# First two tiles of x ahead, a separate buffer of empty rows, and expert weights loaded in eight slices, in a transformer block with eight experts

## The reference: one block of attention and experts

```python
mod = (silu(c) @ wmod)                       # sa, ca, ga, sb, cb, gb per sequence
h = layernorm(x) * (1 + ca) + sa
x = x + ga * attention(h)                    # 16 heads, 4 key/value heads, 64 wide, window of 128,
                                             # scores through 30 * tanh(s / 30)
h = layernorm(x) * (1 + cb) + sb
x = x + gb * experts(h)                      # 8 experts of 128 -> 512 -> 128, each token goes to
                                             # the one with the largest gate, at most 512 per expert
```

## Time and profile before

| | |
|---|---|
| median of 3 runs | 476.98 us (475.44 to 479.21) |
| profiled execution | 476.81 us, span 475.1 us |
| mean granted TensorE clock | 0.952 |
| busy: PE, DVE, ACT, POOL | 88%, 60%, 63%, 65% |
| bytes moved | 37.73 MB, of which written to memory 17.31 MB |

### The profile page before, as it was taken

One profiled execution on the slowest core, in us unless ns is written; L12 is line 12 of the kernel. 1 busy time (PEld: TensorE's weight loads), 2 busy tenths in 40 slices (PEclk: granted clock), 3 DMA queues, 4 the chain that ended last, 5 costly groups with the idle time before them and its releaser, 6 DMA issues. The chain is left out here.

```text
span 475.1 us, 14910 instructions
## 1 busy us (share of the span) xinstructions
PE 417.4 (88%) x5608; PEld 294.0 (62%) x5608; DVE 286.9 (60%) x846; ACT 298.0 (63%) x537; POOL 310.8 (65%) x494
## 2 busy tenths in 40 slices
PE   2894999999999999999999999999999742899970
PEld 1652566766767676666677666767565531799960
DVE  6263557775676868576777756675777541245631
ACT  4785457777776868777777778676756221564420
POOL 6136248587786969687867878676769851055572
PEclk9998899999999999999999999999999765999995
DMA  8987000101101010102011110101020125971110
GB/s 261 369 294 231 3 23 3 41 25 37 52 20 54 20 52 20 43 19 70 20 52 38 35 41 21 52 20 52 21 86 24 42 96 188 364 248 39 33 50 16
DMA packets 32078, 37.73 MB, mean 79 GB/s; under 512 B 3474, under 2 KB 28311, under 8 KB 32008
## 3 DMA queue, kind: packets, MB, share of 16 engines
q1 hardware_dynamic: 28936, 28.22, 19.1%
q0 software_dynamic: 3072, 8.56, 5.0%
HBM read 15.88 MB, written 17.31 MB: 70 GB/s over the span
## 5 line engine op out<-in xcount | busy, mean ns | idle before, releaser
L1185 POOL TENSOR_TENSOR OL<-O,OH 128x512 fp32r<-128x512 f32 x64 | 81.3, 1285 | 22.3 <-ACT OH L701 21.8
L865 DVE COPY_PREDICATED own<-before,turns 128x1024 f32<-128x1024 uint32 x56 | 68.8, 1229 | 40.3 <-PE turns L424 40.3
L689 ACT ACTIVATE PR<-own 128x1024 f32<-128x1024 f32 x64 | 65.5, 1024 | 42.4 <-DVE own L865 42.0
L1177 POOL TENSOR_SCALAR_AFFINE_SELECT PM<-PR 128x1024 f32<-128x1024 f32 x64 | 69.5, 1096 | 22.4 <-ACT PR L695 22.0
L695 ACT ACTIVATE PR<-PR 128x1024 f32<-128x1024 f32 x64 | 65.8, 1054 | 0.0
L420 PE MATMUL own<-Q,K 64*32 64x256 f32 (+3 forms) x896 | 58.8, 441 | 1.9 <-ACT PR L689 1.7
L896 DVE TENSOR_TENSOR O<-turns,R 128x512 f32<-128x512 f32 x64 | 41.2, 685 | 29.2 <-PE turns L463 28.9
L424 PE MATMUL turns<-Q,K 64*32 64x128 f32 (+3 forms) x896 | 57.4, 429 | 0.0
L701 ACT ACTIVATE OH<-O 128x512 fp32r<-128x512 f32 x64 | 40.0, 628 | 11.0 <-DVE O L896 10.9
L1221 POOL DMA_INDIRECT sorted_rows<-PAY,slot_i x32 | 35.1, 1096 | 14.0 <-issue 10.9
L424 PEld LDWEIGHTS turns<-Q,K 64*32 64x32 f32 x896 | 36.5, 107 | 9.4
(11 more groups left out here) (189 smaller groups left out, 1010.8 us busy)
## 6 DMA issues: line engine op xcount, KB each, us to landing
sorted_rows<-PAY SPq DMA_DIRECT2D x8, 800.0 KB, 12.1
VM<-V SPq DMA_DIRECT2D x56, 64.0 KB, 2.1
x_sb<-x_dram SPq DMA_DIRECT2D x4, 512.0 KB, 6.7
w_stage<-w_dram SPq DMA_DIRECT2D x1, 2048.0 KB, 10.9
out_dram<-PAY SPq DMA_DIRECT2D x32, 64.0 KB, 1.7
x_sb<-sorted_rows SPq DMA_DIRECT2D x2, 800.0 KB, 9.6
Q<-sorted_rows SPq DMA_DIRECT2D x2, 800.0 KB, 9.1
PR<-sorted_rows SPq DMA_DIRECT2D x2, 800.0 KB
```

The lines of the kernel that those rows point to most:

```text
L689: act.activation(pr, own[:, :, :].rearrange("p a n -> p (a n)"), ACT.Tanh, scale=SCORE_SCALE).then_inc(tanhed, 1)
L865: dve.copy_predicated(own[:, :, :].rearrange("p a (r n) -> p (a r) n", n=P), before[:, :].bitcast(U32).unsqueeze(1).to_broadcast([P, 2 * R ...
L1177: pool.affine_select(out=PM[:, u % P_RING, :].rearrange("p (r n) -> p r n", n=P), in_=PR[:, u % P_RING, :].rearrange("p (r n) -> p r n", n ...
L1185: pool.tensor_tensor(OL[:, t % 2, c, :], O[:, t % 2, c, :], OH[:, t % 2, c, :].bitcast(F32), ALU.subtract).then_inc(ol_done, 1)
```

## The change

The first batch of x is loaded in two parts, two tiles and six tiles. c and wmod are loaded from ScalarE's queue, wmod in two halves, wq in two halves with a semaphore each. The eight blocks of empty rows are issued ahead of wo and of the other three batches of x, and come from a buffer of their own; a row is 388 words long instead of 400. ScalarE normalises tiles 0 and 1 before it splits the query weights, and VectorE makes the first `XL` before it splits the other half of them and the value weights. The first weights of the experts are loaded in eight transfers of one expert each, one in each turn of SyncE's loop from tile 8 on, instead of one transfer before the loop.

```diff
-ROW_H, ROW_G, ROW_X, ROW_ID, ROW = 0, P, 2 * P, 3 * P, 400
+ROW_H, ROW_ID, ROW_G, ROW_X, ROW = 0, P, P + 4, 2 * P + 4, 3 * P + 4
+W1_TILE = 8
-        empty_row = PAY[:, PAY_RING - 1, :]
+        empty_row = sb("empty_row", [P, ROW])
...
-            sp.dma_start(x_sb[:, 0:BATCH_TILES, :], x_v[0]).then_inc(x_in[0], 16)
-            sp.dma_start(cT[:, :], c).then_inc(c_in, 16)
-            sp.dma_start(stage_m, wmod).then_inc(wmod_in, 16)
+            sp.dma_start(x_sb[:, 0:2, :], x_v[0][:, 0:2, :]).then_inc(x_first, 16)
             sp.dma_start(stage_k, wk).then_inc(wk_in, 16)
+            sp.dma_start(stage_q[:, QH:], wq[:, QH:]).then_inc(wq1_in, 16)
+            sp.dma_start(stage_q[:, :QH], wq[:, :QH]).then_inc(wq0_in, 16)
             sp.dma_start(stage_v, wv).then_inc(wv_in, 16)
-            sp.dma_start(stage_q, wq).then_inc(wq_in, 16)
+            sp.dma_start(x_sb[:, 2:BATCH_TILES, :], x_v[0][:, 2:BATCH_TILES, :]).then_inc(x_in[0], 16)
+            sp.wait_ge(consts, CONSTS)
+            for e in range(EXPERTS):
+                sp.dma_start(sorted_v[e], empty_row[:, :].unsqueeze(1).to_broadcast([P, ST, ROW])).then_inc(empty_in, 16)
+            sp.dma_start(stage_o, wo.rearrange("p (i n) -> p i n", n=P)).then_inc(wo_in, 16)
             for b in range(1, BATCHES):
                 sp.dma_start(x_sb[:, b * BATCH_TILES:(b + 1) * BATCH_TILES, :], x_v[b]).then_inc(x_in[b], 16)
-            sp.dma_start(stage_o, wo.rearrange("p (i n) -> p i n", n=P)).then_inc(wo_in, 16)
             sp.dma_start(Wg[:, :], wg).then_inc(rest_in, 16)
             sp.dma_start(b1_col[:, :, :], b1).then_inc(rest_in, 16)
-            sp.wait_ge(consts, CONSTS)
-            for e in range(EXPERTS):
-                sp.dma_start(sorted_v[e], empty_row.unsqueeze(1).to_broadcast([P, ST, ROW])).then_inc(empty_in, 16)
...
-            sp.wait_ge(weights_l, len(split))
-            sp.wait_ge(columns_done, 1)
-            sp.wait_ge(rows_done, 1)
-            sp.dma_start(w1_sb, w1.rearrange("e h f -> h e f")).then_inc(w1_in, 16)
+
+            def load_w1(e):
+
+                if e == 0:
+                    sp.wait_ge(weights_l, len(split))
+                    sp.wait_ge(columns_done, 1)
+                    sp.wait_ge(rows_done, 1)
+                sp.dma_start(w1_sb[:, e, :], w1[e]).then_inc(w1_in, 16)
...
                 if is_tile(e + 24):
                     mix_v(e + 24)
+                if W1_TILE <= e + 14 < W1_TILE + 2 * EXPERTS:
+                    load_w1((e + 14 - W1_TILE) // 2)
...
+            act.dma_start(cT[:, :], c).then_inc(c_in, 16)
+            act.dma_start(stage_m[:, 0:3 * P], wmod[:, 0:3 * P]).then_inc(wmod_in, 16)
+            act.dma_start(stage_m[:, 3 * P:6 * P], wmod[:, 3 * P:6 * P]).then_inc(wmod2_in, 16)
             act.wait_ge(c_in, 16)
             act.activation(c_e[:, :], cT[:, :], ACT.Exp, scale=-1.0).then_inc(c_exped, 1)
             split_high(SPLIT_K)
+            normalise1(0)
+            normalise1(1)
+            split_high(SPLIT_Q1)
+            high_x(0)
             split_high(SPLIT_Q0)
             split_high(SPLIT_V)
-            split_high(SPLIT_Q1)
...
             def measure1(t):
-                dve.wait_ge(x_in[t // BATCH_TILES], 16)
+                dve.wait_ge(x_first if t < 2 else x_in[t // BATCH_TILES], 16)
...
                 if e == -16:
                     keep_columns()
                     split_low(SPLIT_K)
-                    split_low(SPLIT_Q0)
-                    split_low(SPLIT_V)
                     split_low(SPLIT_Q1)
-                    prepare_mod()
                 if is_tile(e + 16):
                     full_x(e // 2 + 8)
                     low_x(e // 2 + 8)
+                if e == -16:
+                    split_low(SPLIT_Q0)
+                    split_low(SPLIT_V)
+                    keep_gate()
+                    prepare_mod()
...
-            pool.memset(PAY[:, :, :], 0.0).then_inc(consts, 1)
+            pool.memset(PAY[:, :, ROW_ID:ROW_G], 0.0).then_inc(consts, 1)
+            pool.memset(empty_row[:, :], 0.0).then_inc(consts, 1)
...
             def scatter(t):
                 r = t % PAY_RING
+                if t == 0:
+                    pool.wait_ge(empty_in, 16 * EXPERTS)
```

More of the change, by code:

```diff
@@ L46 @@
 HOME = {
-    ("columns",): 0, ("rows",): 1,
+    ("columns",): 0, ("rows",): 2,
     ("before", 0, 0): 2, ("before", 0, 1): 2, ("before", 1, 0): 2, ("before", 1, 1): 1,
@@ L185, in build @@
         turns = pb("turns", [P, 6, 512])
+        x_first = sem("x_first")
         x_in = [sem(f"x_in{b}") for b in range(BATCHES)]
-        wk_in, wv_in, wq_in, c_in, wmod_in, wo_in, w1_in, b2_in, rest_in, mod_in = sems(
-            "wk_in", "wv_in", "wq_in", "c_in", "wmod_in", "wo_in", "w1_in", "b2_in", "rest_in", "mod_in")
+        wk_in, wv_in, wq0_in, wq1_in, c_in, wmod_in, wmod2_in, wo_in, w1_in, b2_in, rest_in, mod_in = sems(
+            "wk_in", "wv_in", "wq0_in", "wq1_in", "c_in", "wmod_in", "wmod2_in", "wo_in", "w1_in", "b2_in", "rest_in", "mod_in")
         mod_out, empty_in, row_rest_in = sems("mod_out", "empty_in", "row_rest_in")
@@ L234, in build @@
         split = (
-            (WkH[:, :], WkL[:, :], stage_k), (WqH[:, :QH], WqL[:, :QH], stage_q[:, :QH]), (WvH[:, :], WvL[:, :], stage_v),
-            (WqH[:, QH:], WqL[:, QH:], stage_q[:, QH:]),
+            (WkH[:, :], WkL[:, :], stage_k), (WqH[:, QH:], WqL[:, QH:], stage_q[:, QH:]),
+            (WqH[:, :QH], WqL[:, :QH], stage_q[:, :QH]), (WvH[:, :], WvL[:, :], stage_v),
             (WoH[:, REP:, :], WoL[:, REP:, :], stage_o[:, REP:, :]), (WoH[:, :REP, :], WoL[:, :REP, :], stage_o[:, :REP, :]))
-        SPLIT_K, SPLIT_Q0, SPLIT_V, SPLIT_Q1, SPLIT_O1, SPLIT_O0 = range(6)
-        split_in = (wk_in, wq_in, wv_in, wq_in, wo_in, wo_in)
-        CONSTS = 14
+        SPLIT_K, SPLIT_Q1, SPLIT_Q0, SPLIT_V, SPLIT_O1, SPLIT_O0 = range(6)
+        split_in = (wk_in, wq1_in, wq0_in, wv_in, wo_in, wo_in)
+        CONSTS = 15
         turn_banks = [turns[:, n, :] for n in (0, 1)]
@@ L532, in program_pe @@
             n, ps = take("rows")
+            pe.wait_ge(wmod2_in, 16)
             pe.matmul(ps[0:BATCHES, 0:3 * P], siluT[:, :], stage_m[:, 3 * P:6 * P], start=True, stop=True).then_inc(rows_done, 1)
@@ L722, in gate_row @@
                     act.wait_ge(mod_in, 16)
-                    act.wait_ge(empty_in, 16 * EXPERTS)
                 if t >= PAY_RING:
@@ L751, in program_act @@
                     keep_h2(e + 6)
-                if is_tile(e + 14):
+                if is_tile(e + 14) and e + 14 > 1:
                     high_x(e // 2 + 7)
@@ L778, in program_act @@
                     expose(e + 11, 1)
-                if is_tile(e + 16):
+                if is_tile(e + 16) and e + 16 > 1:
                     normalise1(e + 16)
-                if is_tile(e + 17):
+                if is_tile(e + 17) and e + 17 > 1:
                     normalise1(e + 17)
@@ L820, in relu @@
                     act.activation(hidden[e % 2][:, f, :], up_banks[f], ACT.Relu, bias=b1_col[:, e, f:f + 1]).then_inc(relu_done, 1)
-            act.wait_ge(w1_in, 16)
+            act.wait_ge(w1_in, 16 * EXPERTS)
             act.wait_ge(rest_in, 32)
@@ L904, in add_x @@
                     dve.wait_ge(x1_out[r], 16 * (t // PAY_RING))
-                elif t == 0:
-                    dve.wait_ge(empty_in, 16 * EXPERTS)
                 dve.tensor_tensor(PAY[:, r, ROW_X:ROW_X + P], bank["y", t][:, 0:P], x_sb[:, t, :], ALU.add).then_inc(x1_done, 1)
@@ L976, in keep_columns, with keep_gate @@
                 dve.tensor_scalar(ca_col[:, :], col[:, 4:4 + BATCHES], 1.0, None, ALU.add).then_inc(ca_kept, 1)
+            def keep_gate():
+                col = bank["columns",]
                 dve.tensor_scalar(ga_sign[:, :], col[:, 8:8 + BATCHES], 0.0, 0.5, ALU.is_ge, ALU.subtract).then_inc(ga_signed, 1)
@@ L1140, in program_pool @@
                                pattern=[[-1, P]], channel_multiplier=1).then_inc(consts, 1)
-            pool.wait_ge(consts, 5)
+            pool.wait_ge(consts, 6)
             pool.memset(empty_row[:, ROW_ID:ROW_ID + 1].bitcast(I32), NO_TOKEN).then_inc(consts, 1)
@@ L1144, in program_pool @@
             pool.iota(tok_id[:, :], pattern=[[P, TILES]], base=0, channel_multiplier=1).then_inc(consts, 1)
-            pool.wait_ge(consts, 10)
+            pool.wait_ge(consts, 11)
             pool.tensor_copy(iota8[:, :], iota8i[:, :]).then_inc(consts, 1)
@@ L1211, in name_row @@
                     pool.wait_ge(pay_out[r], 16 * (t // PAY_RING))
-                else:
-                    pool.wait_ge(empty_in, 16 * EXPERTS)
                 pool.tensor_copy(PAY[:, r, ROW_ID:ROW_ID + 1].bitcast(I32), tok_id[:, t:t + 1]).then_inc(id_done, 1)
```

## The result

The changed kernel takes 484.79 us in the median of 4 runs (482.92 to 485.90), the kernel before on the same occasion 476.21. The ratio is 1.0176, 95% interval 1.0142 to 1.0209: it is slower, by 8.4 us if the ratio is applied to the 476.21. The forecast was 479.6 us and no change; the range ended at 484.5.

The account below looks back on a forecast made before the run. TensorE was taken to bound the attention, so head delays reach the end almost whole. A net +2.6 us at attend(1)'s end plus 0.2 for the slices gave +2.8 on 476.81: 479.6 us, no change, range 470 to 484.5.

Parts of the forecast that it names:

- the wait for VM: TensorE's 6.10 us hole before attend(1), behind the 2 MB load; with its slow clock, 8.7 us were to go.
- the slices: First weights in eight loads during the attention, ahead of VM copies and x1 stores: bounds 0 and 8.9 us, 0.2 taken.
- behind those on TensorE is project_q(1, 2): Head: waiting measure1(8) holds full_x(1) and first merges, then project_q(1, 2), which starts at 30.5 us, 10.0 later.
- the slow clock: TensorE after the hole: twelve matmuls from project_q(1, 2) +1.0 us, scores +1.0 us, with 0.3 as the other end.
- The landing of the second batch: x's second batch, behind eight blocks and wo in SyncE's queue, lands at 28.9 us instead of 9.9.
- ScalarE: Held at the split of wo until 27.2 us, through by 30, and does not set the end.
- Rival D: Attention: slices hold up VM or x1 stores until VectorE, then TensorE wait, half of 8.9 us: 484 us; chance 0.09.
- A: The forecast itself, second batch of x held in the head: 479.6 us, own range 477 to 482.5; chance 0.57.
- First loads: Head: x's rest in at 8.0 us, full_x(0) at 10.9, TensorE's first projection at 12.05, a gain of 1.25 us.
- Rival B: Head: second batch of x isn't held, by overtaking stores or faster blocks; faster, 466.9 us; chance 0.17.
- Rival C: Eight blocks slower because 1,552 bytes are no multiple of 64: 2.55 us a block, +2.9, 482.5 us; chance 0.17.

Follow-up runs that it names:

- after_pitch400: The changed kernel with rows of 400 words again and the whole of PAY cleared at the start: 483.06 us, ratio 1.0121 to the kernel before.
- after_x_ahead: The changed kernel with the second to fourth batch of x ahead of the eight blocks again, wo still behind them: 486.15 us, ratio 1.0189.
- first_block_early: Changed kernel, loads ahead again, slices from tile -6, blocks in SyncE's loop, VectorE's first-block work before measuring tiles 2 to 7: 465.87 us, ratio 0.9779.

## Why the prediction was wrong: the hold caught TensorE a step earlier

The direction was right: the wait for VM goes, and a longer hole in the head takes its place, ended through VectorE by the second batch of x. The size was not: +2.6 us at the end of attend(1) became 57.90 - 51.08 = +6.8, and behind attend(1) 1.4 us were added where 0.2 were booked for the slices. The profiled execution got +8.0 us instead of +2.8. The median, 484.79, is above the 481.8 at which I had let slower begin and 0.3 us above the range.

*The step "behind those on TensorE is project_q(1, 2)" failed.* The hold catches TensorE earlier, at project_v(0). That one needs no new x. But it writes bank 1 of `turns`, the memory for TensorE's results, where turn_x(1) has left its own (`HOME`: both ("x",) and ("v",) are 1), and the bank is free only after low_x(1), VectorE's line at 32.05. So the value projection and the first scores of tile 0, 32.53 to 36.03, lay behind the hole and not ahead of it: +3.5 us. In before they took 1.8 us, 18.71 to 20.50; the slow clock makes up the rest. I had followed the waits written in `project_v` and not those of `take`, which waits until a bank is free. No run gave project_v a bank of its own, so this rests on the program and the trace.

*The landing of the second batch was put too early, 28.9 instead of 31.05 us.* 1.5 us of it is x's rest, in at 9.5 instead of 8.0, and 0.6 us is the pace of the blocks, where the shorter rows saved nothing. In none of the kernels with this order of the first loads did x's rest land before 8.6 us, so 8.0 was too early by 0.6 at least. What makes it 9.5 stays open: it came at 8.6 in after_pitch400, with the blocks directly behind, and at 9.2 in after_x_ahead, with other loads there.

*The slow clock* cost less than booked: the stretch from project_q(1, 2) to attend(1) took 19.0 instead of 20.3 us. The stretch at 0.50 is 32.5 to 37.5 us, and most of it had fallen on the steps ahead of project_q(1, 2). From the landing of the batch to TensorE's start it took 0.1 us less than booked. Together +3.5 + 2.1 - 0.1 - 1.3 = +4.2, the whole difference at the end of attend(1).

*ScalarE* does not set the end in the changed kernel, and so far the prediction was right: its splits of wo were through at 30.5 us, and then it waited 3.75 us for project_v(0). But after_x_ahead shows that its hold alone is as long.

*The slices*: 0.2 booked; the stretch behind attend(1) is 1.4 us longer in this pair of executions, 2.6 by the table, and 0.8 by the medians, which is inside the noise. Rival D had this place with 4.4 us; if it came, it came on top of A in a smaller size. The experts' part is 0.3 us shorter than before.

*First loads*: the gain of 1.25 us at the first projection did not come (13.52 against 13.30), by the late rest of the first batch. It would have been worth nothing behind the hole; the part of the forecast that said the split buys little because VectorE measures tiles 2 to 7 first was right, and first_block_early shows it.

*Rival B* is out: the second batch did not overtake the blocks. It landed at 31.05, 1.7 us behind wo (16.82 + 12.5 = 29.3), in the order of issue. Rival C is out by the 2.3 us a block. By the runs the order costs 14.8 us, the slices and the rest gain 6.4, and 8.4 is the difference.

## What to carry to other kernels

When a transfer is moved back in a queue, list every engine's first instruction that waits for it, and for each what stands behind it in that engine's program, whether it needs the data or not; include the waits for buffers and banks that a held instruction would have freed. Two engines held side by side hide each other: an experiment that frees one of them shows no gain (486.15 and 484.43 against 484.79), and freeing both gives 14.8 us. And a large transfer that nobody needs soon belongs behind the small ones that somebody waits for; whether it is cut matters less than its place.

## What the runs showed of the hardware

The column of the granted clock does not show every slow stretch. From 13.30 to 16.60 us the kernel before reads 1.00, though its matmuls come every 0.21 us, as they do at 0.50 in the changed kernel from 32.5 to 37.5, and every 0.12 us afterwards:

```profile
13.30:16.60 3.30, 3.30 (x15) 3.30 (x16) 0.49 (x3) 0.96 (x2) 1.29 (x4) 1.00 1.06 376
```

A block of 512 rows took 2.2 to 2.3 us at 1,600 bytes a row and 2.3 us at 1,552.
